# A third pair of score stacks, SyncE's order reworked, and x loaded once into a ring of six

## The reference

```
q = layernorm(x) @ Wq.T;  k = ctx @ Wk.T;  v = ctx @ Wv.T      # 32 sub-heads of 8, 16 heads of 16
att = softmax(q k^T / sqrt(8))                                 # per sub-head
att = att[:, :, 0] - lam * att[:, :, 1]                        # the two sub-heads of a head
x = x + att v
h = layernorm(x)
x = x + shared(h) + 2.5 * (two best of 16 experts, weighted)(h)
```

## Time and profile before

| | |
|---|---|
| median of 3 runs | 2260.15 us (2256.93 to 2262.98) |
| the profiled execution's own time | 2249.22 us |
| its span, first to last instruction | 2247.5 us |
| busy in the span | PE 90%, DVE 71%, POOL 64%, ACT 63% |
| attention part | to about 1660 us |
| DMA packets | 616921, of these 447811 under 512 B |
| moved | 432.05 MB, mean 192 GB/s |

### The profile page before, as it was taken

The page is one execution under the profiler, slowest core; times in us unless marked ns, Lnnn a source line. Parts: engine busy times, 40 slices in busy tenths (PEclk is TensorE's granted clock), DMA queues, the critical chain, the costliest instruction groups (busy, mean ns, idle before and its releaser), DMA issues.

```text
span 2247.5 us, 76469 instructions
## 1 busy us (share of the span) xinstructions
PE 2021.7 (90%) x20840; PEld 1405.2 (63%) x20840; DVE 1584.5 (71%) x4623; ACT 1426.2 (63%) x3511; POOL 1446.2 (64%) x2183
## 2 busy tenths in 40 slices
PE   4999999999999999999999999999977988889996
PEld 3666665566656566656656566666546877768775
DVE  3777777777777777778777777778765655546554
ACT  2777777777777777777776777777763444434443
POOL 4466777767677676767676767767664555545554
PEclk8899999999999999999999999999987999999999
DMA  5997777777777777777777777878846777667774
GB/s 133 222 225 192 187 195 190 178 189 184 191 190 184 186 194 185 185 183 182 191 193 178 184 188 190 194 181 216 228 173 180 223 214 214 199 178 220 220 223 127
DMA packets 616921, 432.05 MB, mean 192 GB/s; under 512 B 447811, under 2 KB 562634, under 8 KB 616400
## 3 DMA queue, kind: packets, MB, share of 16 engines
q1 hardware_dynamic: 556528, 319.91, 58.3%
q0 software_dynamic: 32256, 84.47, 11.8%
q10 hardware_dynamic: 28000, 26.03, 3.8%
HBM read 234.59 MB, written 197.72 MB: 192 GB/s over the span
## 4 chain that ended last, share of the span: by engine, by line
PE 67%; DVE 15%; issue 10%; ACT 3%; DMA 2%; SPq 1%; POOL 1%; DVEq 1%; another core or an unknown queue 1%; ACTq 0%; POOLq 0%
PE mx_ps L494 11%; PE o_ps L527 7%; DVE mx L982 6%; PE ms_ps L778 5%; PE o_ps L538 5%; PE ms_ps L555 5%; PE mx_ps L557 4%; PE mx_ps L555 4%; PE ms_ps L576 4%; PE st_ps L756 3%; PE mx_ps L556 3%; PE ms_ps L583 3%; PE st_ps L487 3%; PE ms_ps L556 3%; PE ms_ps L557 2%
## 5 line engine op out<-in xcount | busy, mean ns | idle before, releaser
L982 DVE TENSOR_REDUCE mx<-mx_ps 128x4 f32<-128x512 f32 x1024 | 686.3, 685 | 300.4 <-PE mx_ps L494 294.2
L826 ACT ACTIVATE prob<-st_ps 128x512 f32<-128x512 f32 x1024 | 604.5, 598 | 357.8 <-PE st_ps L487 353.5
L494 PE MATMUL mx_ps<-stacks 48*128 48x128 bf16 x4096 | 396.7, 221 | 67.6 <-DVE mx L982 33.8
L487 PE MATMUL st_ps<-stacks 50*128 50x128 bf16 x4096 | 394.9, 220 | 0.0
L494 PEld LDWEIGHTS mx_ps<-stacks 48*128 48x128 bf16 x4096 | 230.9, 95 | 228.6 <-issue 105.9
L527 PE MATMUL o_ps<-prob,v_sb 128*32 128x256 f32 x4096 | 331.6, 396 | 0.8 <-ACT prob L826 0.4
L1344 POOL DMA_INDIRECT rows_dram<-rowt,posi x256 | 253.7, 991 | 67.6 <-issue 64.3
L555 PE MATMUL ms_ps<-e_lo 128*128 128x256 f32 x768 | 264.7, 345 | 18.1 <-issue 11.1
L923 ACT ACTIVATE rows_T<-st_ps 128x256 fp32r<-128x256 f32 x288 | 111.7, 388 | 192.2 <-PE st_ps L756 137.3
L487 PEld LDWEIGHTS st_ps<-stacks 50*128 50x128 bf16 x4096 | 229.8, 95 | 2.5 <-issue 1.5
L1413 POOL DMA_INDIRECT sums_dram<-stacks x144 | 141.7, 984 | 130.4 <-DVE stacks L1220 70.2
(11 more groups left out here) (155 smaller groups left out, 4694.4 us busy)
## 6 DMA issues: line engine op xcount, KB each, us to landing
stack_dram<-w_dn_sb SPq DMA_DIRECT2D x768, 128.0 KB
stacks<-stack_dram SPq DMA_DIRECT2D x512, 192.0 KB
stacks<-rows_dram SPq DMA_DIRECT2D x288, 130.0 KB
w_dn_sb<-in_x SPq DMA_DIRECT2D x64, 256.0 KB
w_dn_sb<-in_ctxT SPq DMA_DIRECT2D x64, 256.0 KB
x_res<-in_x SPq DMA_DIRECT2D x64, 256.0 KB
stacks<-sums_dram SPq DMA_DIRECT2D x78, 128.0 KB
stacks<-base_dram SPq DMA_DIRECT2D x76, 128.0 KB
```

The lines of the kernel that those rows point to most:

```text
L487: return pe.matmul(st_ps[k % 2][:, i * P:(i + 1) * P], k_st[p][64 * h:64 * h + KROWS, u, j, :], q_st[p][64 * h:64 * h + KROWS, u, j, :], s ...
L494: return pe.matmul(mx_ps[k % 2][:, i * P:(i + 1) * P], q_st[p][64 * h:64 * h + ROWS, u, j, :], k_st[p][64 * h:64 * h + ROWS, u, j, :], sta ...
L826: nc.scalar.activation(prob[k % 4][:, :], st_ps[k % 2][:, :], ACT.Exp, scale=float(HALF) ** -0.5).then_inc(a_exp, 1)
L982: v.tensor_reduce(mx[:, u, c * CHUNK:(c + 1) * CHUNK], mx_ps[k % 2][:, :].rearrange("p (c n) -> p c n", c=CHUNK), AX.X, ALU.max).then_inc( ...
```

## The change

It does six things.

1. A third pair of stacks lies in the space of the experts' weights `e_hi`. The pairs are used in turns of three, and all of a pair is loaded at once, in step n2 - 2, when the scores of step it - 1 are done.
2. `stack_dram` has another layout: 4 copies instead of 6 are written, in rows of 512 B, and the stack's last two copies are read a second time from them. So there are eight puts of 128 KB per step instead of twelve, and still eight loads: per stack and half, one of 256 KB (32 rows) and one of 128 KB (16 rows). The loads alternate between the partition halves h = 1 and h = 0.
3. PE waits for stacks twice per step instead of four times.
4. SyncE's order is another. Behind the key puts and the context load come all eight loads, then x, and `put_max(b, 0)` is last.
5. x is loaded once, five steps ahead, into a ring of six buffers, from which norm and residual both read.
6. The loop has six steps to a round, so 9 rounds. On PE its body has 1578 instructions where it had 546, 167 of them register work (REGISTER_ALU) where it had 71; on DVE 565 where it had 201, on ACT 428 for 155, on POOL 246 for 93.

```diff
-COPIES = 6
-Q_COPIES, K_COPIES = (0, 1, 2, 0, 1, 0), (0, 1, 0, 1, 0, 2)
+COPIES = 4
+Q_COPIES, K_COPIES = (0, 1, 2, 0), (2, 0, 0, 1)
+Q_AGAIN, K_AGAIN = 0, 2
...
-    stack_dram = nc.dram_tensor("stack_dram", (2, 2, 2, 2, COPIES, HALF, SHH, P), BF16, kind="Internal").ap()
+    stack_dram = nc.dram_tensor("stack_dram", (2, 2, 2, COPIES, HALF, SHH, SW), BF16, kind="Internal").ap()
...
-        q_st, k_st = [stack(0), stack(2)], [stack(1), stack(3)]
+        q_st, k_st = [stack(2), stack_of_experts(0), stack(0)], [stack(3), stack_of_experts(1), stack(1)]
...
-        x_res = [sb(f"x_res{i}", [P, 2, D]) for i in range(2)]
+        x_in = [sb(f"x_in{i}", [P, 2, D]) for i in range(6)]
...
-            pipeline(eng, body, first, lo, hi, end, 2)
+            pipeline(eng, body, first, lo, hi, end, 6)
...
+            def load_stacks(s):
+
+                p, i = s.par(), s.third()
+                for n, buf, again in ((0, q_st[i], Q_AGAIN), (1, k_st[i], K_AGAIN)):
+                    for row, copy, m in ((0, 0, COPIES), (COPIES * HALF, again, 2)):
+                        for h in (1, 0):
+                            sp.dma_start(buf[64 * h + row:64 * h + row + m * HALF, :, :].rearrange("p j w -> p (j w)"),
+                                         stack_dram[p, n, h, copy:copy + m].rearrange("r d j w -> (r d) (j w)"),
+                                         max_dma_last_dim=4096).then_inc(d_stk[h][p], 16)
...
-                if b.is_in(0, NS):
-                    wait(sp, p_st, NCH, it)
-                    wait(sp, p_mx, NCH, b)
-                    load_stacks(b, 1, 1)
-                    load_stacks(b, 1, 0)
...
-                    load_stacks(n2, 0, 1)
+                    load_stacks(n2)
+                x5 = it.plus(5)
+                if x5.is_in(1, NS):
+                    wait(sp, g_x2, 4, it, 0)
+                    sp.dma_start(x_in[x5.sixth()][:, :, :],
+                                 x_g[bass.ds(x5.idx(), 1)].rearrange("g p u d -> (g p) u d")).then_inc(d_x[x5.par()], 16)
                 if b.is_in(0, NS):
                     put_max(b, 0)
-                if n2.is_in(0, NS):
-                    load_stacks(n2, 0, 0)
...
                 if do_b:
-                    if k % 4 == 0:
-                        wait(pe, d_stk[u][1 - k // 4 % 2], STK, b, STK)
+                    if k in (0, 4):
+                        wait_par(pe, d_stk[1 - k // 4], STK, b)
...
-            for i in range(2):
-                g.memset(k_st[i][:, :, :, :], -1.0).then_inc(g_ones, 1)
+            for i in range(3):
+                g.memset(k_st[i][:, :, :], -1.0).then_inc(g_ones, 1)
...
                 if h == 0:
-                    wait_par(gp, d_res, 16, s)
+                    wait_par(gp, d_x, 16, s)
```

More of the change, by code:

```diff
@@ L57, in par, with sixth, third @@
         return self.off % 2
+    def sixth(self):
+        return self.off % 6
+    def third(self):
+        return self.off % 3
     def pair(self):
@@ L143, in program @@
         ahead = w_dn_sb[:, :, :].rearrange("p e d -> p (e d)")
-        x_in, xn = (ahead[:, i * 512:(i + 1) * 512].rearrange("p (u d) -> p u d", u=2) for i in range(2))
+        xn = ahead[:, 0:512].rearrange("p (u d) -> p u d", u=2)
         c_in = ahead[:, 1024:1536].rearrange("p (k t) -> p k t", k=DK)
@@ L218, in program @@
         hid_T = [v_sb[0][:, i * P:(i + 1) * P] for i in range(4)]
-        d_w, d_x, d_c = sem("d_w"), sem("d_x"), sem("d_c")
+        d_w, d_c = sem("d_w"), sem("d_c")
         a_wh, v_wl, v_x, a_ch, g_cl = sem("a_wh"), sem("v_wl"), sem("v_x"), sem("a_ch"), sem("g_cl")
-        d_res = [sem(f"d_res{i}") for i in range(2)]
+        d_x = [sem(f"d_x{i}") for i in range(2)]
         d_qw, d_kw = sem("d_qw"), sem("d_kw")
-        d_stk = [[sem(f"d_stk{u}{h}") for h in range(2)] for u in range(2)]
+        d_stk = [[sem(f"d_stk{i}{h}") for i in range(2)] for h in range(2)]
         d_m = [sem(f"d_m{i}") for i in range(2)]
@@ L270, in program @@
         first, lo, hi, end = -4, 4, NS - 6, NS + 3
+        assert (hi - lo) % 6 == 0 and (NS - 1) % 3 == 0
         PAD_STEPS = (*range(lo), *range(hi, hi + 4))
@@ L347, in _, with put_parts @@
                 sp.dma_start(lam_in[:, n, :], src.partition_broadcast(P)).then_inc(d_w, 16)
[L349 to L363, removed]
+            def put_parts(s, n, part, landed, copies):
+                for h in range(2):
+                    wait_par(sp, d_stk[h], STK, s.plus(-2))
+                for i, r in enumerate(copies):
+                    sp.dma_start(stack_dram[s.par(), n, :, i].rearrange("h d j w -> (d j) h w"),
+                                 part[:, r, :].rearrange("p (h w) -> p h w", h=2)).then_inc(landed, 16)
+            def load_stacks(s):
[6 more added lines that the diff above has]
+                                         max_dma_last_dim=4096).then_inc(d_stk[h][p], 16)
             def put_max(s, u):
@@ L369, in put_max @@
                     row = 64 * h + ROWS
-                    sp.dma_start(q_st[s.par()][row:row + 2, u, :, :],
+                    sp.dma_start(q_st[s.third()][row:row + 2, :, u * P:(u + 1) * P],
                                  mxT[u][2 * SHH * h:2 * SHH * (h + 1), :]).then_inc(d_m[u], 16)
@@ L862, in step @@
                     if k == 7 and do_xs:
-                        wait(act, d_x, 16, xs, 16)
+                        wait_par(act, d_x, 16, xs)
                         wait(act, p_xT, 1, xs)
-                        norm(xs, x_in, mv1, nb1, xn, g_nb1, a_n1)
+                        norm(xs, x_in[xs.sixth()], mv1, nb1, xn, g_nb1, a_n1)
                     if k == 11 and do_b:
@@ L1123, in step @@
                     if k == 2 and do_xs:
-                        wait(dve, d_x, 16, xs, 16)
-                        stats(xs, x_in, bs1, mv1, v_b1, v_s1, a_n1)
+                        wait_par(dve, d_x, 16, xs)
+                        stats(xs, x_in[xs.sixth()], bs1, mv1, v_b1, v_s1, a_n1)
                     if k == 4 and do_d:
```

42 lines of the change are left out of this document (18 added, 24 removed).

## The result

The changed kernel takes **2448.3 us** (median of 4 runs, 2444.15 to 2455.35), the kernel before, on the same chip, 2258.93: ratio **1.0839**, 95% interval 1.0805 to 1.0873. The prediction (2335, slower) had the direction and one of the two causes, the late put; the other, the form of the loop, it had put at nothing. It was 113 us short and its range ended at 2390.

What follows compares the result with a forecast made beforehand. PE, 90% busy, was taken to bound the kernel; the late put would add +50 us in the loop, +11, +4 and +3 ahead and +7 behind, together +75 on 2260.15: 2335 us, forecast range 2268 to 2390, overall 2236 to 2390.

Steps and rivals of the forecast that it cites:

- So the loads are hidden in the loop, and a load that comes sooner gains nothing there.: Loop: no stack load stands among PE's long waits, so earlier loads were claimed to gain nothing.
- Keys at +11.6, first load at +15.25: SyncE's chain, in us from a step's first scores: keys ready at +11.6, unchanged; first load after four puts and landing.
- I take 195, near the low end: 9.4 us.: Load queue: 1.83 MB ahead of the put at 195 GB/s, between ends of 182 and 295, takes 9.4 us.
- the fixed 1.3 and 0.44: Chain to the next step: 1.3 us fixed part of a transfer; 0.3 for the put and 0.14 to PE.
- my 26.4: Loop step set by the late put_max(b, 0): claimed 26.4 us instead of 25.47.
- Fewer waits and jumps: Loop: less PE register work per step and 8 jumps back for 26, counted as nothing since PE waits anyway.
- where I had 50: Loop term of the sum: 54 steps at 26.4 instead of 25.47 us, +50 us.
- +11, +4 and +3: Ahead of the loop: four steps +11 us, the first stacks +4, the step that follows +3.
- +7: Behind the loop: four steps that still load stacks, 26.4 instead of 24.7 us each, +7 us.
- Rival 1: Loop: put lands before +25.2 us and fewer jumps and registers make the loop lighter; 2242 us, chance 0.28.
- Rival 2: Loop: larger body fetched anew each round, 1.1 to 2.5 us each; about no change, 2258 us, chance 0.12.
- What would show it: Trace signs: PE waits about 1 us for mxT, marks 26 to 27 us apart, DMA share near 60%.

Runs made afterwards that it cites:

- e7: Changed kernel with put_max(b, 0) between the upper-half and lower-half loads, all steps written out without a hardware loop: 2195.36 us, 0.9756 of the kernel before.
- r6: Repeat of e7, changed kernel with put_max(b, 0) between the half loads and all steps written out: 2203.14 us, 0.9748 of the kernel before.
- e8: Changed kernel with its own SyncE order, all steps written out on all engines: 2348.08 us, 1.0443 of the kernel before.
- r1: Changed kernel run again on the faster kind of chip: 2343.07 us, 1.1357 of the kernel before (2065.39 us there).
- r2: Repeat of e8, changed kernel written out on all engines, on the faster kind of chip: 2254.69 us, 1.0918 of the kernel before.
- e6: Kernel before with all 67 attention steps written out, no hardware loop: 2179.62 us, 0.9701 of the kernel before.
- r4: Changed kernel written out on all engines plus 24 filler matmuls per step ahead of PE's waits, faster kind of chip: 2227.10 us, 1.0770 of the kernel before.
- e1: Changed kernel with put_max(b, 0) moved between the upper-half and lower-half loads, loop kept: 2317.48 us, 1.0267 of the kernel before.
- e4: Kernel before with six steps to a loop round instead of two, nothing else changed: 2291.69 us, 1.0178 of the kernel before.
- after: The changed kernel itself, as measured against the kernel before: 2448.30 us, ratio 1.0839.
- e2: Changed kernel with only the x load moved behind put_max(b, 0): 2364.77 us, 1.0488 of the kernel before.
- e12: Kernel before with only PE's steps written out, on the faster kind of chip: 2084.22 us, 1.0099 of the kernel before.

## Why the prediction was wrong, step by step

- **"So the loads are hidden in the loop, and a load that comes sooner gains nothing there."** Right: e7 and r6.
- **Keys at +11.6, first load at +15.25: "PE's and ACT's pace sets this; the change leaves it."** Not so. From a step's first scores to the issue of the first load it is 16.02 us in the changed kernel (mean of the 54 steps) and 14.74 in e8, without a loop. The new form of the loop moved it by 1.28 us; against the forecast it came 0.8 us late, 42 us in the loop.
- **"I take 195, near the low end: 9.4 us."** Too fast. The loads alone ran at 171 GB/s, under my low end of 182. From the first load to the next first scores e8 takes 26.66 - 14.74 = 11.92 us for my 11.15, 0.8 us a step or some 42 us; less the fixed 1.3 and 0.44 this is 1.83 MB at 180 GB/s, the row that I had passed over for 195. A step without any loop takes 26.66 us for my 26.4, only 0.26 x 54 = 14 us more, because its first load comes 0.5 us before my +15.25, which was read from a kernel with a loop. That the two nearly cancel is luck.
- **"Fewer waits and jumps: ... Nothing, since PE waits for the put anyway."** This is the step that failed. The loop's form adds 28.46 - 26.66 = 1.80 us to a step that waits for the put, 54 x 1.80 = 97 us (r1 against r2, on one chip: 1.51 us, 82 us).

  Of the 1.80, 1.3 come between a step's first scores and the first load, ahead of the put, and 0.5 behind the first load. A wait covers only what runs beside it. PE's pause at the jump ended 2.2 us after mxT had landed in the step shown, fetches ran beside the very loads that the put waits for, and the register work of PE, on whose pace the keys hang, and of SyncE, which issues the puts, the loads and x between the keys and the put, lies on the chain to the put. Of the 97 us, 9 x 3.6 = 32 are the excess of the steps with a jump (31.46 against 27.86), the rest is spread over all steps. How that rest divides among register work, fetches inside the body and the clock (141 us of e8's loop at half clock, 247 of the changed kernel's) was not tested; PE itself has no fewer instructions written out, 609 a step in e8 for 594 (register work gone, more semaphore rows).

  And I subtracted 25.47 as if it were all work: e6 shows that 1.18 us of it was the old loop's form, so the late put itself cost 54 x (26.66 - 24.29) = 128 us and the new form 54 x (1.80 - 1.18) = 34 more than the old. Together 162, as measured (161.5), where I had 50: 50 + 14 + 97 = 161. The split holds for the slower kind of chip.
- **Ahead of and behind the loop.** +11, +4 and +3 were +27.8, and +7 was +13.3: the same order, each too small. The stretch from 65 to 156 us shows why in part, a clock of 0.86 for 0.95.
- **The clock** was not in the sum. It has no term of its own in the split above, since it stands inside the 26.66 and the 1.80; r4 puts its price there, without a loop, at 28 us net of the filler's own work, on the other kind of chip.
- **Rival 1** asked for a put in time. e1 gave it that and was still 1.0267, so its "loop gets lighter" was wrong in sign: nine long rounds cost more than 27 short ones (e4).
- **Rival 2** had the cause, fetches at each round, and a price, 1.1 to 2.5 us each, that is too low: e4 measured 4.1, even net of the jumps saved. "Under my forecast it hides in the wait" is the same mistake as above.
- **What would show it.** PE's wait for mxT, the chain and the DMA share (0.59) came as named. The wait is 69.1 us over 28 waits, 2.5 us each and not 1; the marks stand 28.5 us apart and not 26 to 27. "SyncE hardly waits for ACT's mxT" was wrong: it waits 268.8 us for it from 400 to 1500, at the u = 1 put, which it now reaches early. The wait is not on the chain of the step shown, where SyncE waits for the keys behind it.

## What to carry to other kernels

In a queue that works in order, a small transfer that the next step waits for goes ahead of the large ones that are needed later; 256 KB ahead of it cost 3.5% here (after against e2). A cost counts as hidden by a wait only if it is not on the chain that ends the wait: ask which engines and queues make the awaited thing, and whether the cost slows them too. And a loop body that is fetched anew at each round costs more than its jumps did when it was short (e4); where the program can be written out, measure that first, on each kind of chip that it will run on (e6 against e12).

## What the runs showed of the hardware

- A jump back in a long body cost about 4 us a round (e4), and PE, DVE and ACT stood together over it (after, 858.2 to 865.5 us). With the two-step body, some 1210 instructions on PE, no instruction packet moved from 400 to 1500 us; with six steps, some 3570, PE's fetches ran all through the loop (e4: 111 packets of q8).
- After a pause of 7.3 us PE ran at half clock for more than 6 us; filling pauses with matmuls nobody needs made the kernel 28 us faster (r4 against r2).
- Written out, the kernel before gained 71 us although PE had been at 93% of the loop: a busy share near full did not mean that no time was left in it (e6).
- The kernel before took 2064 us on one chip and 2250 to 2260 on the others. Behind the loop the changed kernel took 638 us there (r1) and 729 elsewhere, so a good part of that lies in the experts' half; the cause was not looked into.
